# First attention: the maxima of the next unit dealt over other halves, and their split moved two halves later

## The reference, cut to what matters

```
x = x + L0_attn(layernorm(x));  seven more sub-layers follow, none of them touched
L0_attn: B=2, S=1024, D=128, 16 heads of 8; qkv = x @ w_attn + b_attn
    scores = (q @ k^T) * 8**-0.5 + mask,  mask = -log(delta + 1) for delta = key - query > 0,
                                          0 on the diagonal, -inf for keys before the query
    out = softmax(scores) @ v, then @ w_proj + b_proj
```

## Time and profile before

| what | us |
| --- | --- |
| median of 3 runs (lowest to highest) | 1101.44 (1099.18 to 1110.61) |
| the profiled execution | 1102.42 |
| its span | 1100.3 |
| units 0 to 7 of the first attention, in the span | 73.4 to about 385 |

### The profile page before, as it was taken

How to read it: one execution, slowest core, us unless ns; L and a number is a source line. 1 busy time by engine, 2 the same in 40 slices (tenths; PEclk the granted TensorE clock), 3 DMA queues, 4 the chain that set the end, 5 groups by cost and what they waited for, 6 DMA issues and landing times. The chain is left out here.

```text
span 1100.3 us, 17965 instructions
## 1 busy us (share of the span) xinstructions
PE 896.0 (81%) x6334; PEld 606.8 (55%) x6334; DVE 665.8 (61%) x1876; ACT 427.8 (39%) x1024; POOL 512.2 (47%) x463
## 2 busy tenths in 40 slices
PE   4668999999999867267899699994998987389992
PEld 2122333333333356155566588994895756389982
DVE  6767778686872075879687656778003666533334
ACT  2323665565666441113111276774334211032220
POOL 5425888888898831053222344555200001156661
PEclk9657999899999988758799799997999998599997
DMA  4800110110000000001000000302000001266764
GB/s 146 257 1 1 31 31 2 30 30 19 13 2 24 1 22 8 0 15 40 1 2 1 10 21 10 134 9 77 1 1 1 1 10 30 89 188 216 217 196 145
DMA packets 38893, 55.95 MB, mean 51 GB/s; under 512 B 6954, under 2 KB 26290, under 8 KB 38678
## 3 DMA queue, kind: packets, MB, share of 16 engines
q1 hardware_dynamic: 36310, 49.70, 14.9%
q0 software_dynamic: 2496, 5.12, 1.6%
HBM read 43.66 MB, written 10.94 MB: 50 GB/s over the span
## 5 line engine op out<-in xcount | busy, mean ns | idle before, releaser
L423 POOL TENSOR_TENSOR arena<-arena 128x1024 f32<-128x1024 f32 (+3 forms) x105 | 201.0, 1946 | 42.4 <-ACT arena L598 42.3
L665 DVE CUSTOM_DVE_ANT_0 ps<-ps,arena 128x512 f32<-128x512 f32 (+3 forms) x256 | 148.7, 640 | 45.3 <-PE ps L480 44.4
L598 ACT ACTIVATE arena<-ps 128x512 f32<-128x512 f32 (+3 forms) x320 | 137.3, 491 | 89.4 <-PE ps L511 58.1
L480 PE MATMUL ps<-arena 48*128 48x512 bf16 (+3 forms) x384 | 103.9, 371 | 24.9 <-DVE arena L665 15.9
L117 POOL TENSOR_SCALAR vareps<-meanvar 128x4 f32<-128x4 f32 x32 | 7.9, 246 | 213.2 <-DVE meanvar L98 213.2
L503 PE MATMUL ps<-arena 51*128 51x512 bf16 (+3 forms) x384 | 76.0, 349 | 6.0 <-DMA arena<-arena 5.2
L2075 PE MATMUL ps<-arena 128*128 128x128 f32 x624 | 79.9, 284 | 0.0
L480 PEld LDWEIGHTS ps<-arena 48*128 48x128 bf16 x384 | 28.3, 95 | 91.3 <-DVE arena L665 55.1
L2075 PEld LDWEIGHTS ps<-arena 128*128 128x128 f32 x624 | 76.4, 200 | 0.0
L152 PE MATMUL ps<-ident,xn 128*128 128x128 f32 x128 | 26.0, 352 | 59.4 <-DVE x L921 19.9
L532 PE MATMUL ps<-arena 128*9 128x512 f32 (+3 forms) x640 | 67.7, 495 | 3.9 <-POOL arena L423 3.9
(11 more groups left out here) (341 smaller groups left out, 2081.0 us busy)
## 6 DMA issues: line engine op xcount, KB each, us to landing
arena<-in_L_ffn_w SPq DMA_DIRECT2D x39, 512.0 KB, 3.7
arena<-scratch SPq DMA_DIRECT2D x32, 192.0 KB, 4.0
arena<-in_L_ffn_w SPq DMA_DIRECT2D x16, 256.0 KB, 3.4
scratch<-arena SPq DMA_DIRECT2D x12, 256.0 KB, 4.4
arena<-expert_rows SPq DMA_DIRECT2D x8, 256.0 KB, 4.9
scratch<-arena SPq DMA_DIRECT2D x4, 384.0 KB, 5.0
scratch<-arena SPq DMA_DIRECT2D x12, 128.0 KB, 4.3
x<-in_x SPq DMA_DIRECT2D x4, 256.0 KB, 3.9
```

Source lines behind the costliest of these rows:

```text
L423: nc.gpsimd.tensor_tensor(e, e, weight[:, at:at + k].unsqueeze(1).broadcast_to([P, 2, k]), ALU.mult).then_inc(weighed, 1)
L480: nc.tensor.matmul(m.ps[:, (2 * k + e) % MAX_BANKS, 0:wd], qs[rows, u % BUFS, pair, i * P:(i + 1) * P], ks[rows, u % BUFS, pair, first:fir ...
L598: nc.scalar.activation(probs(g)[:, 2 * p + e, 0:wd], m.ps[:, BANK[h, e], 0:wd], ACT.Exp, scale=SCALE).then_inc(exps, 1)
L665: nc.vector.tensor_tensor_reduce(out=scores, in0=scores, in1=before[:, 0:wd], scale=-1.0, scalar=negrest[:, h, i:i + 1] if i < TPC else 3e ...
```

## The change

The margin between the end of a window and the unit's own h0 goes from 10 halves to 8, for every unit. The price of a half, by which the pieces are dealt, was 2 ns per column plus 300 ns; it now has a smaller slope and a surcharge for log halves. The price of a piece was the same line for far and near pieces; it now has two lines. Which halves GpSimd weighs is unchanged (two functions only move up in the file).

```diff
+    MARGIN = 8
     def window(u):
-        return (0, HALVES - 10) if u == 1 else ((u - 1) * HALVES - 10, (u - 1) * HALVES + HALVES - 10)
+        return (0 if u == 1 else (u - 1) * HALVES - MARGIN), u * HALVES - MARGIN
+
+    def tensor_time(h):
+        wd = width(h // 2 % NG)
+        return 200 + 1.4 * wd + (0 if h in BY_POOL else 1.7 * wd)
+
+    def vector_time(n):
+        wd = piece_width(n)
+        return 2 * (100 + 1.0 * wd if PIECES[n][0] == "far" else 260 + 1.1 * wd)
 
     def pieces_at():
         at = {}
         for u in range(1, UNITS):
             first, end = window(u)
-            span = [2 * width(h // 2 % NG) + 300 for h in range(first, end)]
-            cost = [2 * piece_width(n) + 150 for n in range(NP)]
+            span = [tensor_time(h) for h in range(first, end)]
+            cost = [vector_time(n) for n in range(NP)]
```

More of the change, by code:

```diff
@@ L262, in l0_attn @@
     HALVES = 2 * NG
-    def window(u):
-        return (0, HALVES - 10) if u == 1 else ((u - 1) * HALVES - 10, (u - 1) * HALVES + HALVES - 10)
[L267 to L270, removed]
-            span = [2 * width(h // 2 % NG) + 300 for h in range(first, end)]
-            cost = [2 * piece_width(n) + 150 for n in range(NP)]
[L273 to L283, removed]
     def diagonal(n):
@@ L303, in l0_attn, with window, pieces_at @@
     POOL_COUNT = list(itertools.accumulate(h in BY_POOL for h in range(UNITS * HALVES)))
+    def window(u):
+        return (0 if u == 1 else (u - 1) * HALVES - MARGIN), u * HALVES - MARGIN
[5 more added lines that the diff above has]
+        return 2 * (100 + 1.0 * wd if PIECES[n][0] == "far" else 260 + 1.1 * wd)
+    def pieces_at():
+        at = {}
+        for u in range(1, UNITS):
+            first, end = window(u)
+            span = [tensor_time(h) for h in range(first, end)]
+            cost = [vector_time(n) for n in range(NP)]
+            n = spent = gone = 0
+            for h, t in zip(range(first, end), span):
+                gone += t
+                while n < NP and (spent + cost[n] / 2) * sum(span) <= gone * sum(cost):
+                    at.setdefault(h, []).append((u, n))
+                    spent += cost[n]
+                    n += 1
+            assert n == NP
+        return at
+    PIECES_AT = pieces_at()
     def schedule():
```

## The result

The changed kernel takes 1156.17 us (median of 6 runs, 1152.96 to 1159.58). Six runs of the kernel before beside it, three of them new, have a median of 1111.11 (1099.18 to 1114.33). On the same chips the ratio of the two is 1.0447, 95% interval 1.0405 to 1.0488: slower, as forecast, but the time lies above the range (1111 to 1152), and the loss, 45 us by the medians and 49 by the ratio, is well above the 34 that the sum had. Some executions of any version are longer at a lower granted clock; all ratios here leave them out, nine of the twelve of the run warm among them, and the profile of by_trace is of such an execution. The profiled execution took 1159.58, its span 1157.5.

What follows compares the result with a forecast made beforehand. No engine is full; a unit takes TensorE's steps plus its waits, with GpSimd's 31.8 us as floor. 1102.4 + 28.8 (standstills at the split) + 10 (clock) - 5 (deal) = 1136 us, range 1111 to 1152.

Steps and rivals of the forecast that it cites:

- the sum: Whole kernel: 1102.4 + 28.8 (split) + 10 (clock) - 5 (pieces dealt otherwise) = 1136 us.
- What bounds a unit: First attention: a unit's time is TensorE's steps plus its waits, 36.7 us at full clock; GpSimd's 31.8 is the floor.
- The split meets h16 and h17: Before turn_max, units 0 to 5: the CAST waits for GpSimd's two weighings, TensorE stands still; 6 x 4.8 = 28.8 us.
- This CAST waits through the border: Split's first VectorE instruction: waits until GpSimd is idle, through both weighings of h16 and h17, ending at T + 6.6.
- Rival B: At h16: the CAST slips in between the weighings, turn_max starts 2.4 us earlier; 1114 us in all, chance 0.08.
- The clock: Behind the six standstills: granted clock falls to 0.50, 2.4 us each time at most; 6 x 1.6 = 10 us, ends 0 and 15.
- two thirds: Share taken of the 2.4 us clock loss per standstill, as part of the slow stretch lies under take_max.
- The deal: h0 to h5: fewer pieces, 0.6 us a unit in units 1 to 5, 2 in unit 0; -5 us, ends 0 and -12.
- Rival D: h0 to h5, VectorE full: the even deal pays, 14 us in all, if no standstill; 1092 us, chance 0.10.
- The rows' way: Rows in at T + 13.3, next h0 at T + 15.4: 2 us of slack, costs nothing.

Runs made afterwards that it cites:

- warm: split_first with extra, unread matmuls of 512 columns in the first maxima and 18 behind the first turn_max; ratio to the kernel before 1.0081.
- by_trace: split_first with the halves' prices taken from durations measured in unit 7 of the kernel before; ratio to the kernel before 1.0059.
- fill: The changed kernel with 18 extra, unread matmuls ahead of turn_max in units 0 to 5; ratio to the kernel before 1.0170.
- split_first: The changed kernel with the split of the maxima ahead of piece 0 at h16, not behind it; ratio to the kernel before 0.9979, repeated 0.9992.
- short_weigh: The changed kernel with GpSimd weighing only 16 columns of h16 and h17 in units 0 to 5; ratio to the kernel before 0.9973.
- cast_act: The changed kernel with the split's first instruction, the CAST, made by ScalarE instead of VectorE; ratio to the kernel before 1.0404.
- only_prices: The changed kernel with the margin back at 10 halves, so the new prices alone; ratio to the kernel before 1.0059.
- only_margin: The kernel before with the margin of 8 halves alone, at the old prices; ratio to the kernel before 1.0530.
- fill_half: The changed kernel with 9 extra, unread matmuls ahead of turn_max in units 0 to 5; ratio to the kernel before 1.0341.

## Why the prediction was right in sign and wrong in size

- **What bounds a unit: right.** TensorE's steps plus its waits; the busy times of ScalarE and GpSimd in units 0 to 5 hardly moved (22.0 to 22.7 and 31.1 to 32.1).
- **The split meets h16 and h17: right in place, and the price came out.** Six units, not the seventh; forecast 28.8 us, measured 26.0 in the waits and 26.0 between fill and split_first. split_first and short_weigh show the cause from both ends.
- **"This CAST waits through the border": wrong inside, and that the sum did not suffer was luck.** In all six units the CAST took 2.09 us and got in after one weighing, then the subtraction took 2.24 and waited for the other. The end is the same, the second weighing's, but by a second lock that I had not thought of. Rival B had the first half right and priced it as if the rest of the split were free; cast_act shows that it is not. The rule of the Trainium skill, which I had set against the row, was right at this place. It does not fit what led me away from it: the CASTs of units 2 and 6 before passed a border of two short weighings, and so did that of unit 5 (2.54 us) and that of unit 6 in only_prices:

```profile
340.43 2.52 POOL L433 TENSOR_TENSOR xnT<-xnT,arena 128x512 f32<-128x512 f32 x2
...
340.40 2.65 DVE L685 CAST arena<-arena 128x32 bf16<-128x32 f32 x1
```

  All four were beside two weighings of 1.3 us; all 24 CASTs beside two of 2.3 us (six each in changed, only_margin, fill and fill_half) got in after the first. Why stays open.
- **The clock: the step that failed.** I had "6.8 and 6.5 us" of half clock behind a standstill, from two places outside the attention, times two thirds, times 0.36, six times: 10 us, at most 15. Measured: 23.4 behind the standstills, and 5.9 more in unit 0 ahead of them. The rate was near (0.30 against 0.36); the duration was not. The six slow stretches are 17, 17, 6.8, 17, 17 and 6.8 us long, 82 us in all: two as I had taken them, four two and a half times that. And the two thirds had no ground: after them the sum has 4.5 us for each, where 12 was measured from turn_max on (73 us in six; the rest of the 82 lies inside the standstills). Two instances in other layers were taken for a constant, though the same rows held a stretch of 10.1 us in unit 3.
- **The deal: -5 forecast, -6.6 in the profile of split_first (266.0 against 272.6), -1 to -2 by its ratios, zero within their intervals.** In h0 to h5 VectorE's share fell as forecast, 5.51 busy of 6.3 us (0.87) in unit 2 of the changed kernel, and the six halves from 7.9 to 6.3 us, near the ceiling of 1.75 (by stretches: h0 to h5 of unit 2, then h6 to h15 of the changed kernel); the whole unit kept 0.9 of it in split_first (36.7 to 35.8). The -6.6 is not the deal's alone: split_first ran 17 us less at half clock than the kernel before, worth about 5 us by an estimate at 0.30 each. Rival D was right about that place and wrong that it matters.

```profile
182.40:188.70 6.30, 5.53 (x51) 1.79 (x50) 5.51 (x17) 5.70 (x12) 4.72 (x3) 1.00 0.15 40
188.70:206.00 17.30, 16.18 (x114) 6.39 (x112) 11.79 (x46) 8.97 (x22) 17.30 (x9) 1.00 0.01 2
```

- **The rows' way: right.** No unit after unit 0 waited for its rows, with the wait or, in split_first, without it.
- **The sum again:** 1102.4 + 26.0 + 29.3 - 6.6 = 1151.1; up to unit 7 it closes by construction, as its terms are differences of the same stretches. The remaining 8.5 of the profiled execution lie behind unit 7's start (763.1 against 754.3), in layers whose order is unchanged; ten other profiles have 749.6 to 764.7 there, so I count them as scatter. Without them and without the 5.9 in unit 0 the change costs 42.8 us, near the 45 of the medians.
- **The range.** Part of the miss is the starting point: I began from 1102.4, and the kernel before had a median of 1111.11 in the runs beside the changed one. The ratio times 1101.4 would be 1150.7, just inside. The loss is above the 34 of the sum either way.

## What to carry to other kernels

An order can be right in every wait it was planned for and still fall on a resource that is in no plan: before moving a small VectorE instruction on data in SBUF, look at what GpSimd does at the new place, instruction by instruction, for each has to take its own turn. A standstill of TensorE has two prices, its length and the slow stretch behind it, and here the second (23 us) was about as large as the first (26); take it from as many places as the trace has, and from the same kind of work, with its longest case in the range. Where a standstill can't be avoided, spare matmuls in it can be the cheaper way, if the clock is up when they begin (fill, against warm).

## What the runs showed of the hardware that was not expected

- The granted clock stayed at 0.50 for 15 us behind a standstill of 4.3 us, with TensorE busy 98% of it, and for more than 18 us in warm with TensorE busy throughout. A busy TensorE by the profile is not enough to get the full clock back soon.
- A pause of 2.3 us (fill_half) cost about three fifths of what one of 4.3 us did, both counted above fill: ratio 1.034 against 1.045, and 1.017 with a pause of 0.36 us (fill); the stretches have 310.8 against 321.3 and 292.0 us.
- The clock also fell without a standstill: it was at half for 10.1 us in unit 3 before, with TensorE busy 10.04, and in the 7 us ahead of that TensorE was never idle for more than 0.6 us at a time.
- A subtraction of 128x32 elements with two inputs in SBUF took 2.06 to 2.24 us beside a GpSimd multiplication of 128x1024, and 0.22 without it; a conversion on ScalarE took 0.34 to 0.35 us in all eight units, in seven of which such a multiplication began in the middle of it.
